# A new order of the TensorE step in a gated linear attention layer with a routed expert MLP

## The chip, the cores and the metric

The kernel is one program on one core of a Trainium2 chip. Its time is the device time of one execution in microseconds, the median of three runs. A profiled execution has its own time, and the span of its trace is a little shorter than that time.

## The reference

The input x holds 32 sequences of 256 tokens of 128 features. Each row is normalised, and two branches are added to it: a gated linear attention, and an MLP of which each token uses one expert of eight.

```
xn = layernorm(x)
q, k = xn @ Wq, xn @ Wk                 # 4 heads of 32
v, g = xn @ Wv, xn @ Wg                 # 4 heads of 64
gk   = log_sigmoid(xn @ Wgk + bgk) / 16 # one decay per token and head
o    = chunked gated linear attention of q, k, v, gk (causal, with a state per head)
on   = o * rsqrt(mean(o*o) + 1e-5) * gnorm_w
attn = (on * silu(g)) @ Wo
e    = argmax(softmax(xn @ gate_w))
ffn  = probability[e] * (gelu(xn @ w1[e] + b1[e]) @ w2[e] + b2[e])
out  = x + attn + ffn
```

## The kernel before, in words

The program is written engine by engine: each of the five engines has its own instruction list, in the order in which the source calls its helpers, and semaphores tie the lists together. Nothing is scheduled by a compiler.

There are three stages. The first loads x, transposes it and works out decays, router logits and the table that sorts tokens by expert. The second, the attention, takes one sequence a step, s = 0 to 31, in a pipeline over several steps. The third runs 71 blocks of 128 sorted rows through the MLP: TensorE multiplies, VectorE (`weigh`) makes the result and GpSimd adds it to the output rows by an indirect DMA with accumulation (`scatter`, L619). GpSimd starts its first scatter when the 32 attention results (`res`) have landed in the output, since it waits for `res_stored`.

In step s TensorE works on three sequences at once: Q and K (`proj_qk`, psQK) and V and G (`proj_vg`, psVG) of s+1; the transposed first keys (`first_keys`), the scores, the state and the outputs of s; the transposes of the normed outputs (`transpose_on`, psT) of s-1 and the last projection (`project_out`, psT) of s-2. Matmuls are fp32, so most of them appear as two records each; Q, K, V and G are three fp32r products each.

The scores of the four heads are four matmuls of 32 rows side by side. Two heads write psA and two write the first halves of psVG's two banks. So `scores(s)` waits until VectorE has read G of s out of psVG (`gate_ready`), and `proj_vg(s+1)`, which comes after it and overwrites psVG, waits until VectorE has read those scores (`p_ready`). The steps 6 to 29 are a loop of the sequencer with two steps in its body (L953).

ScalarE squares the outputs of s-1, copies the transposes of s-2, makes the eight decay tiles E of s+1 (`exp_dec`), copies Q and K of s+1, and then takes tanh of G and copies V. VectorE makes `gate`, `x_lo` (the low parts of x for s+2), the mean squares `ms` and `msn`, the masked scores `pr` (`probs`), the decayed keys `kd`, the gated outputs `og`, the scaled queries `qe`, the normed outputs `on`, the state `S_sb` and the residual `res`. GpSimd takes the power -1/2 (`rms`), masks E of s+1 (`mask_dec`, L554) once `on` of s-1 is made, and between these places sorted rows by indirect DMAs, two or three a step in the steps 5 to 29 (L577). SyncE issues the loads of decays and the stores of results.

In the last step, s = 31, the MLP's first blocks are mixed in, and the expert numbers are read into VectorE's registers (`value_load`, L1678).

Of the kernel before, what the change touches and what calls it, by code (L numbers as in the profile page):

```python
# [63 lines left out]
def build_layer(nc, x, Wq, Wk, Wv, Wg, Wgk, bgk, Wo, gnorm_w, gate_w, w1, b1, w2, b2, out):  # L64
# [40 lines left out]
    with ExitStack() as ctx:  # L105
# [99 lines left out]
        qk_sb = sb("qk_sb", [P, 2 * SEQ])  # L205
        kT = qk_sb[:, SEQ:2 * SEQ]
# [29 lines left out]
        psKS = ps("psKS", [P, 512])  # L236
        psA = ps("psA", [P, 2, 512])
        psO = ps("psO", [P, 512])
# [106 lines left out]
        BY_HALVES = (0, 1, LAST)  # L345
        HEADS_IN_TURN = (2, 3, 0, 1)
        ps_pair = [psA, psVG]
# [291 lines left out]
        def _(pe):  # L639
# [120 lines left out]
            def proj_vg(i, j):  # L760
                s = i * 2 + j
                parts = [(x_hi[j], w_hi), (x_hi[j], w_lo), (x_lo[j], w_hi)]
                if not (isinstance(i, int) and s == 0):
                    pe.wait_ge(v_copied, s)
                    pe.wait_ge(th_ready, s)
                    pe.wait_ge(gate_ready, s)
                    if not (isinstance(i, int) and s - 1 in BY_HALVES):
                        pe.wait_ge(p_ready, (s - 1) * 2 + 1)
# [5 lines left out]
            def first_keys(i, j):  # L774
                s = i * 2 + j

                pe.wait_ge(qk_copied, s + 1)
                nc.tensor.transpose(psKS[:, 0:P], kT[:, 0:P], ident[:]).then_inc(k0_ready, 1)


            def scores(i, j):
                s = i * 2 + j
                pe.wait_ge(p_ready, s * 2)
                pe.wait_ge(gate_ready, s + 1)
                if isinstance(i, int) and s == SLOTS_AT + 1:
                    pe.wait_ge(slot_read, 2)
                for k in range(2):
                    for h in HEADS_IN_TURN:
                        rows_h = slice(h * DK, (h + 1) * DK)
                        last = nc.tensor.matmul(ps_pair[h // 2][:, h % 2, k * P:(k + 1) * P], kT[rows_h, k * P:(k + 1) * P], qk_sb[rows_h, k * P:(k + 1) * P],  # L790
# [5 lines left out]
            def scores_by_halves(i, j):  # L796
# [3 lines left out]
                for k in range(2):  # L800
                    for r in range(2):
                        rows_r = slice(r * 2 * DK, (r + 1) * 2 * DK)
                        last = nc.tensor.matmul(psA[:, r, k * SEQ:(k + 1) * SEQ].rearrange("p (b t) -> p b t", b=2), kT[rows_r, k * P:(k + 1) * P], qb[rows_r, :, k * P:(k + 1) * P],
# [4 lines left out]
            def state(i, j):  # L808
# [3 lines left out]
                pe.wait_ge(v_copied, s + 1)  # L812
                for c in range(2):
                    last = nc.tensor.matmul(psKS[c * 2 * DK:(c + 1) * 2 * DK, HV:HV + 2 * DV], kd[:, c * 2 * DK:(c + 1) * 2 * DK],  # L814
# [3 lines left out]
            def own_half(i, j, k):  # L818
                s = i * 2 + j
                if k == 0:  # L820
                    pe.wait_ge(p_ready, (s + 1) * 2)
                for h in range(H):
                    for c in range(2):
                        t = k * SEQ + h % 2 * P + c * P // 2
                        nc.tensor.matmul(psO[c * P // 2:(c + 1) * P // 2, k * HV + h * DV:k * HV + (h + 1) * DV], pr[:, h // 2, t:t + P // 2],  # L825
                                         v_sb[j][:, k, h * DV:(h + 1) * DV], start=(k == 0 and h == 0), stop=False,
                                         skip_group_check=True)

            def outputs(i, j):
# [4 lines left out]
                own_half(i, j, 0)  # L834
                own_half(i, j, 1)
# [26 lines left out]
            def project_out(i, j):  # L862
                s = i * 2 + j
                pe.wait_ge(oT_copied, s + 1)
                for k in range(2):
                    for a in range(2):
                        last = nc.tensor.matmul(psT[:, k * D:(k + 1) * D], oT[:, 2 * k + a, :], wo_sb[:, a, :],  # L867
# [3 lines left out]
            def step(i, j, extra=None, ahead_of_outputs=None):  # L871
                first_keys(i, j)
                proj_qk(*turn(i, j, 1, 2))
                scores(i, j)
# [3 lines left out]
                proj_vg(*turn(i, j, 1, 2))  # L878
# [4 lines left out]
                transpose_on(*turn(i, j, -1, 2))  # L883
# [63 lines left out]
            transpose_on(0, 0)  # L947
# [5 lines left out]
            with pe.Fori(3, SEQS // 2 - 1) as i:  # L953
# [52 lines left out]
            scores_by_halves(last, 1)  # L1006
# [12 lines left out]
            project_out(last, 0)  # L1019
# [3 lines left out]
            project_out(last, 1)  # L1023
# [13 lines left out]
        def _(act):  # L1037
# [758 lines left out]
```

## Time and profile before

| what | us |
| --- | --- |
| median of three runs (389.52 to 390.5) | 389.59 |
| profiled execution | 389.28 |
| span of its trace | 387.5 |
| TensorE busy | 373.4 (96%) |
| VectorE busy | 314.5 (81%) |
| ScalarE busy | 291.8 (75%) |
| GpSimd busy | 279.1 (72%) |

Times in the rows are microseconds from the start of the span, and PE, DVE, ACT and POOL are TensorE, VectorE, ScalarE and GpSimd. Ends of matmuls are modelled in the profile, and matmuls overlap, so the time of a group of matmuls is best read from its start to the start of the next group; a busy TensorE is not one at its peak. What ended an engine's idle time stands in brackets.

### The profile page before, as it was taken

How to read it: one execution, taken by the hardware profiler on the slowest of the kernel's cores; microseconds unless marked ns; L12 is line 12 of the kernel's file. 1: busy time of each engine (PE TensorE's matmuls, PEld its weight loads, DVE VectorE, ACT ScalarE, POOL GpSimd, SP SyncE). 2: the span in 40 equal slices, each digit the busy share in tenths (PEclk: the TensorE clock that was granted, in tenths of full speed). 3: DMA queues.
4: the chain of work that ended last, by engine and by line, in shares of the span. 5: the costliest groups of instructions: out<-in, count | busy, mean ns of one | idle time of the engine just before them, and what ended most of it. 6: DMA issues, size and time to landing. Idle time of an engine off the chain costs nothing.

```text
span 387.5 us, 13901 instructions
## 1 busy us (share of the span) xinstructions
PE 373.4 (96%) x3963; PEld 321.2 (83%) x3963; DVE 314.5 (81%) x859; ACT 291.8 (75%) x889; POOL 279.1 (72%) x245
## 2 busy tenths in 40 slices
PE   7999999999999999999999999899999999999992
PEld 7667777777777877787777877899999999999991
DVE  5988999989898988888888878777788787777761
ACT  4889987788888888888888886566666667666661
POOL 8003534878787888888788873288888888888886
PEclk9999999999999999999999999999999999999997
DMA  8946788456555445575654423155555455556440
GB/s 231 257 140 198 223 270 292 134 170 191 170 184 161 138 147 157 158 200 162 191 157 150 131 79 81 54 67 72 64 72 70 65 70 71 69 71 76 75 37 6
DMA packets 59106, 51.45 MB, mean 133 GB/s; under 512 B 7200, under 2 KB 51392, under 8 KB 59072
## 3 DMA queue, kind: packets, MB, share of 16 engines
q1 hardware_dynamic: 45936, 42.07, 38.8%
q0 software_dynamic: 12272, 8.54, 15.3%
q10 hardware_dynamic: 864, 0.40, 0.4%
q8 instruction: 20, 0.33, 0.4%
q14 instruction: 14, 0.11, 0.1%
HBM read 33.14 MB, written 18.30 MB: 133 GB/s over the span
## 4 chain that ended last, share of the span: by engine, by line
PE 83%; DVE 4%; DMA 3%; issue 3%; ACT 2%; POOL 2%; SPq 2%; DVEq 0%; ACTq 0%; POOLq 0%
PE psA L988 16%; PE psVG L976 15%; PE psVG L771 11%; PE psT L867 8%; PE psO L825 7%; PE psQK L757 5%; PE psT L851 4%; PE psVG L790 4%; PE psO L839 3%; PE psKS L814 3%; POOL out_dram L619 2%; SPq L355 2%; DMA x_all<-in_L_attn_x_dram 1%; ACT E L1160 1%; DMA gcB<-decay_rows 1%
## 5 line engine op out<-in xcount | busy, mean ns | idle before, releaser
L619 POOL DMA_INDIRECT out_dram<-yw,sidx x71 | 112.9, 1590 | 28.8 <-DVE sidx L1700 17.5
L1160 ACT ACTIVATE E<-gcB,ngc 128x128 f32<-128x128 f32 x256 | 78.3, 395 | 0.7 <-DMA gcB<-decay_rows 0.7
L577 POOL DMA_INDIRECT sorted_rows<-x_all,pos_i x64 | 64.9, 1015 | 13.4 <-issue 12.8
L561 POOL TENSOR_TENSOR rms<-msn,neg_half 128x8 f32<-128x8 f32 x32 | 54.4, 1699 | 26.5 <-DVE msn L1492 22.5
L554 POOL TENSOR_SCALAR_AFFINE_SELECT E<-E 128x1024 f32<-128x1024 f32 x32 | 35.2, 1099 | 36.5 <-ACT E L1160 24.9
L1142 ACT ACTIVATE th<-psVG,x_all 128x256 f32<-128x256 f32 x64 | 26.9, 470 | 20.4 <-issue 11.6
L988 PE MATMUL psA<-xT_all,v_sb 128*128 x288 | 38.3, 276 | 1.0 <-issue 0.6
L976 PE MATMUL psVG<-xgT,gcB 128*128 128x128 f32 x288 | 37.9, 275 | 0.0
L988 PE MATMUL psA<-xT_all,th 128*128 x280 | 37.4, 276 | 0.0
L976 PE MATMUL psVG<-xgT,E 128*128 128x128 f32 x280 | 37.0, 275 | 0.0
L867 PE MATMUL psT<-wo_sb,oT 128*128 128x128 f32 x256 | 36.9, 287 | 0.0
L825 PE MATMUL psO<-v_sb,pr 128*64 128x64 f32 x1024 | 35.4, 222 | 1.0 <-DVE pr L1521 0.8
L988 PEld LDWEIGHTS psA<-xT_all,v_sb 128*128 128x128 f32 x288 | 35.0, 192 | 1.4 <-issue 1.4
L825 PEld LDWEIGHTS psO<-v_sb,pr 128*64 128x64 f32 x1024 | 34.1, 138 | 1.6 <-issue 1.5
L976 PEld LDWEIGHTS psVG<-xgT,gcB 128*128 128x128 f32 x288 | 35.0, 192 | 0.0
L988 PEld LDWEIGHTS psA<-xT_all,th 128*128 128x128 f32 x280 | 34.0, 192 | 0.3 <-issue 0.2
L976 PEld LDWEIGHTS psVG<-xgT,E 128*128 128x128 f32 x280 | 34.1, 192 | 0.0
L867 PEld LDWEIGHTS psT<-wo_sb,oT 128*128 128x128 f32 x256 | 31.0, 191 | 3.7 <-issue 0.2
L1169 ACT ACTIVATE sq<-psO 128x512 f32<-128x512 f32 x32 | 19.2, 600 | 13.8 <-PE psO L839 12.5
L771 PE MATMUL psVG<-w_hi,x_hi 128*128 128x512 f32 x64 | 28.2, 441 | 0.9 <-DVE pr L1526 0.6
L1563 DVE SCALAR_TENSOR_TENSOR gate<-th,psVG 128x512 f32<-128x512 f32 x32 | 22.0, 688 | 8.1 <-issue 4.6
L1704 DVE TENSOR_SCALAR yw<-yb,xg 128x128 f32<-128x128 f32 x71 | 26.1, 368 | 2.5
(214 smaller groups left out, 950.6 us busy)
## 6 DMA issues: line engine op xcount, KB each, us to landing
gcB<-decay_rows SPq DMA_DIRECT2D x32, 512.0 KB
sorted_rows<-blank SPq DMA_DIRECT2D x12, 396.0 KB, 5.0
xg<-sorted_rows SPq DMA_DIRECT2D x71, 66.0 KB
x_all<-in_L_attn_x_dram SPq DMA_DIRECT2D x16, 256.0 KB, 5.2
out_dram<-res SPq DMA_DIRECT2D x32, 128.0 KB
eqB<-decay_exp_rows SPq DMA_DIRECT2D x32, 64.0 KB
w1b<-in_L_ffn_w_dram SPq DMA_DIRECT2D x8, 256.0 KB
xT_all<-in_L_ffn_w_dram SPq DMA_DIRECT2D x32, 64.0 KB
```

Source lines behind the costliest of these rows:

```text
L554: nc.gpsimd.affine_select(out=E[j][:], in_=E[j][:], pattern=[[0, 2 * H], [1, P]], compare_op=ALU.is_ge, fill=0.0, base=0, channel_multipli ...
L561: nc.gpsimd.tensor_tensor(rms[j][:], msn[j][:], neg_half[:, 0:2 * H], ALU.pow).then_inc(rms_ready, 1)
L577: nc.gpsimd.indirect_dma_start(out=sorted_dram, out_offset=bass.IndirectOffsetOnAxis(ap=pos_i[:, t:t + 1], axis=0), in_=x_all[:, t, :], in ...
L619: nc.gpsimd.indirect_dma_start(out=out_rows, out_offset=bass.IndirectOffsetOnAxis(ap=sidx[j][:], axis=0), in_=yw[j][:], in_offset=None, bo ...
L771: last = nc.tensor.matmul(psVG[:, k, :], xp[:, k * P:(k + 1) * P], wp[:, 2 * P:], start=(n == 0), stop=(n == 2))
L825: nc.tensor.matmul(psO[c * P // 2:(c + 1) * P // 2, k * HV + h * DV:k * HV + (h + 1) * DV], pr[:, h // 2, t:t + P // 2], v_sb[j][:, k, h * ...
L867: last = nc.tensor.matmul(psT[:, k * D:(k + 1) * D], oT[:, 2 * k + a, :], wo_sb[:, a, :], start=(a == 0), stop=(a == 1))
L976: last = nc.tensor.matmul(psVG[:, j % 2, c * P:(c + 1) * P], wbuf[j % 4][:, c * P:(c + 1) * P], xgT[j % 2][:], start=True, stop=True)
L988: last = nc.tensor.matmul(psY[j % 2][:, 0:D], hid[j % 2][:, c, :], w2_sb[:, bass.ds(e, 1), c, :].rearrange("p a d -> p (a d)"), start=(c = ...
L1142: last = nc.scalar.activation(th[:, k, :], psVG[:, k, HV:2 * HV], ACT.Tanh, scale=x_all[:, bass.ds(s * 2 + k, 1), D + 2:D + 3].rearrange(" ...
L1160: last = nc.scalar.activation(E[j][:, k, h * P:(h + 1) * P], gcB[j][:, k * H + h, :], ACT.Exp, bias=ngcf[:, bass.ds((s * 2 + k) * H + h, 1)])
L1704: c_y.up(nc.vector.tensor_scalar(yw[j][:], yb[j % 2][:], xg[j][:, D:D + 1], None, ALU.mult))
```

## The change

TensorE's step gets another order. Transposes of normed outputs move from the end of the step to behind Q and K and take the sequence s-2 there, one step later than before. V and G come ahead of the scores. The scores leave psVG: psKS and psO become the two banks of one tensor psKO, and the pair of heads that wrote psVG now writes the second half of each of those two banks, the other pair the first halves of psA. The state moves to columns 128 to 255 of psKS. Q and K get two buffers in SBUF.

So the waits move as well. `proj_vg` no longer waits for `p_ready`. `scores(s)` waits for `og` of s-1, for the state copy of s-1 and for `kd` of s, which read the banks that it writes. `state(s)` waits for the first half of `pr`, and `outputs(s)` does the two pairs of heads one after the other, each behind its half of `pr`.

`project_out` is cut in halves of 64 columns of the stationary operand, so it has eight matmuls for four; in the last two sequences the old form stays (`project_whole`). The loop over TensorE's steps 6 to 29 is written out. Step 31 uses the ordinary scores.

VectorE and ScalarE get orders to match: VectorE makes `og` and `kd` ahead of `ms`, and `S_sb` ahead of `on`; ScalarE copies Q and K right behind the squares, and makes E in two halves, one on each side of tanh and V. The first two expert numbers are read in step 30 instead of behind it.

The first place is TensorE's step in the loop of before, the first instruction of each group with its waits (keys, Q and K, scores, projection, V and G, state, outputs of the own chunk, outputs from the state, transposes):

```order
L778 MATMUL psKS<-ident,qk_sb 128x128 [waits qk_copied]
L757 MATMUL psQK<-x_hi,w_hi 128x256 [waits qk_copied,qe_ready,lo_ready,hi_ready]
L790 MATMUL psVG<-qk_sb 128x128 [waits gate_ready,p_ready]
L867 MATMUL psT<-wo_sb,oT 128x128 [waits oT_copied]
L771 MATMUL psVG<-w_hi,x_hi 128x512 [waits p_ready]
L814 MATMUL psKS<-v_sb,kd 64x128 [waits v_copied,kd_ready]
L825 MATMUL psO<-v_sb,pr 64x64 [waits p_ready]
L839 MATMUL psO<-S_sb,qe 64x256 [waits qe_ready,s_copied]
L851 MATMUL psT<-ident,on 128x128 [waits res_ready,dve_on]
```

The same place now:

```order
L776 MATMUL psKO<-ident,qk_sb 128x128 [waits qk_copied]
L757 MATMUL psQK<-x_hi,w_hi 128x256 [waits qk_copied,qe_ready,lo_ready,hi_ready]
L855 MATMUL psT<-ident,on 128x128 [waits res_ready,dve_on]
L769 MATMUL psVG<-w_hi,x_hi 128x512 [waits gate_ready,th_ready,v_copied]
L790 MATMUL psKO<-qk_sb 128x128 [waits s_copied,kd_ready,og_ready,p_ready]
L872 MATMUL psT<-wo_sb,oT 64x128 [waits oT_copied]
L816 MATMUL psKO<-v_sb,kd 64x128 [waits p_ready,v_copied,kd_ready]
L826 MATMUL psKO<-v_sb,pr 64x64 [waits p_ready,og_ready]
L843 MATMUL psKO<-S_sb,qe 64x256 [waits qe_ready,s_copied]
```

Transposes and V and G now stand between Q and K and the scores, and only the projection is left between the scores and the state.

The second place is VectorE's step 9, the last before its own loop (which keeps the same order). Before:

```order
L1563 SCALAR_TENSOR_TENSOR gate<-th,psVG 128x512 [waits th_ready,v_copied]
L1348 TENSOR_TENSOR x_lo<-xT_all,x_hi 128x256 [waits hi_ready]
L1488 TENSOR_REDUCE ms<-sq 128x8 [waits sq_ready]
L1492 SCALAR_TENSOR_TENSOR msn<-ms,vpe 128x8 [waits rms_ready,dve_ms]
L1526 TENSOR_TENSOR pr<-psVG,E 128x2x2x128 [waits a_ready,o_ready,e_masked]
L1526 TENSOR_TENSOR pr<-psA,E 128x2x2x128 [waits a_ready]
L1532 TENSOR_TENSOR kd<-psKS,e_k 128x128 [waits k0_ready]
L1538 TENSOR_TENSOR og<-psO,gate 128x512 [waits sq_ready]
L1511 TENSOR_TENSOR qe<-psQK,eqB 128x128 [waits o_ready,qk_copied,eqB_loaded0]
L1546 TENSOR_TENSOR on<-og,rms 128x512 [waits oT_ps_ready,rms_ready,og_ready]
L1554 TENSOR_TENSOR S_sb<-psKS,headmask 128x256 [waits o_ready,s_ready]
L1571 TENSOR_TENSOR res<-psT,x_all 128x256 [waits res_stored1,wo_ready]
```

Now:

```order
L1587 SCALAR_TENSOR_TENSOR gate<-th,psVG 128x512 [waits th_ready,v_copied]
L1370 TENSOR_TENSOR x_lo<-xT_all,x_hi 128x256 [waits hi_ready]
L1562 TENSOR_TENSOR og<-psKO,gate 128x512 [waits dve_on,sq_ready]
L1554 TENSOR_TENSOR kd<-psKO,e_k 128x128 [waits k0_ready]
L1510 TENSOR_REDUCE ms<-sq 128x8 [waits sq_ready]
L1514 SCALAR_TENSOR_TENSOR msn<-ms,vpe 128x8 [waits rms_ready,dve_ms]
L1533 TENSOR_TENSOR qe<-psQK,eqB 128x128 [waits o_ready,qk_copied,eqB_loaded0]
L1548 TENSOR_TENSOR pr<-psKO,E 128x2x2x128 [waits a_ready,o_ready,e_masked]
L1548 TENSOR_TENSOR pr<-psA,E 128x2x2x128 [waits a_ready]
L1578 TENSOR_TENSOR S_sb<-psKO,headmask 128x256 [waits o_ready,s_ready]
L1570 TENSOR_TENSOR on<-og,rms 128x512 [waits oT_ps_ready,rms_ready,og_ready]
L1595 TENSOR_TENSOR res<-psT,x_all 128x256 [waits res_stored1,wo_ready]
```

`og` and `kd` stand ahead of the masked scores, `ms` behind them both, and the state ahead of `on`.

The diff, cut to its core:

```diff
@@ setup
-        qk_sb = sb("qk_sb", [P, 2 * SEQ])
-        kT = qk_sb[:, SEQ:2 * SEQ]
+        qk_sb = [sb(f"qk_sb{j}", [P, 2 * SEQ]) for j in range(2)]
+        kT = [t[:, SEQ:2 * SEQ] for t in qk_sb]
...
-        psKS = ps("psKS", [P, 512])
+        psKO = ps("psKO", [P, 2, 512])
+        psKS, psO = psKO[:, 0, :], psKO[:, 1, :]
         psA = ps("psA", [P, 2, 512])
-        psO = ps("psO", [P, 512])
...
-        BY_HALVES = (0, 1, LAST)
+        BY_HALVES = (0, 1)
-        ps_pair = [psA, psVG]
+        ps_scores = [psA[:, :, 0:SEQ], psKO[:, :, SEQ:2 * SEQ]]
@@ tensor
             def scores(i, j):
                 pe.wait_ge(p_ready, s * 2)
-                pe.wait_ge(gate_ready, s + 1)
+                pe.wait_ge(og_ready, s)
+                pe.wait_ge(s_copied, s)
+                pe.wait_ge(kd_ready, s + 1)
...
             def state(i, j):
                 pe.wait_ge(kd_ready, s + 1)
                 pe.wait_ge(v_copied, s + 1)
+                if not (isinstance(i, int) and s in BY_HALVES):
+                    pe.wait_ge(p_ready, s * 2 + 1)
...
             def outputs(i, j):
-                own_half(i, j, 0)
-                own_half(i, j, 1)
+                first, second = (0, 1) if isinstance(i, int) and s in BY_HALVES else (1, 0)
+                pe.wait_ge(p_ready, s * 2 + 1)
+                own_pair(i, j, first, True)
+                pe.wait_ge(p_ready, s * 2 + 2)
+                own_pair(i, j, second, False)
...
             def project_out(i, j):
                 for k in range(2):
                     for a in range(2):
+                        for c in range(2):
+                            last = nc.tensor.matmul(psT[c * P // 2:(c + 1) * P // 2, k * D:(k + 1) * D], oT[:, 2 * k + a, c * P // 2:(c + 1) * P // 2],
+                                                    wo_sb[:, a, :], start=(a == 0), stop=(a == 1), skip_group_check=True)
...
             def step(i, j, extra=None, ahead_of_outputs=None):
                 first_keys(i, j)
                 proj_qk(*turn(i, j, 1, 2))
+                transpose_on(*turn(i, j, -2, 2))
+                proj_vg(*turn(i, j, 1, 2))
                 scores(i, j)
                 project_out(*turn(i, j, -2, 2))
                 if extra:
                     extra()
-                proj_vg(*turn(i, j, 1, 2))
                 state(i, j)
                 if ahead_of_outputs:
                     ahead_of_outputs()
                 outputs(i, j)
-                transpose_on(*turn(i, j, -1, 2))
...
-            transpose_on(0, 0)
...
-            with pe.Fori(3, SEQS // 2 - 1) as i:
+            for i in range(3, SEQS // 2 - 1):
...
             first_keys(last, 1)
-            scores_by_halves(last, 1)
+            scores(last, 1)
+            transpose_on(last - 1, 1)
@@ scalar, step
+                if inside(i, j, 1, SEQS):
+                    copy_qk(*turn(i, j, 1, 2))
                 if inside(i, j, -2, SEQS):
                     copy_oT(*turn(i, j, -2, 2))
                 if inside(i, j, 1, SEQS):
-                    exp_dec(*turn(i, j, 1, 2))
-                    copy_qk(*turn(i, j, 1, 2))
+                    exp_half(*turn(i, j, 1, 2), 0)
...
                     tanh(*turn(i, j, 1, 2))
                     copy_v(*turn(i, j, 1, 2))
+                    exp_half(*turn(i, j, 1, 2), 1)
@@ vector
-            step(last, 0)
+            step(last, 0, aside=load_first_experts)
...
-            dve.wait_ge(w_loaded, W_LOADS * 16)
-            e0, e1 = expert_of(0, 0), expert_of(0, 1)
+            e0, e1 = first_experts
```

## Rows read from the trace of the kernel before

**Rows 1.** The page: chain that ended last, shares of the span by engine.

```profile
PE 83%; DVE 4%; DMA 3%; issue 3%; ACT 2%; POOL 2%; SPq 2%; DVEq 0%; ACTq 0%; POOLq 0%
```

**Rows 2.** Windows: stretch in us, its length, busy time of each engine, clock, DMA.

```profile
78.50:228.30 149.80, 149.37 (x1865) 118.89 (x1864) 129.54 (x277) 126.28 (x344) 122.23 (x105) 1.00 0.56 163
```

**Rows 3.** Timeline of TensorE, one step and a half: start, length, engine, line, what, count.

```profile
130.45 0.27 PE L778 MATMUL psKS<-ident,qk_sb 128*128 128x128 f32 x1
130.48 0.36 PE L757 MATMUL psQK<-x_hi,w_hi 128*128 128x256 f32 x1
...
132.03 1.16 PE L867 MATMUL psT<-wo_sb,oT 128*128 128x128 f32 x8
133.13 0.50 PE L771 MATMUL psVG<-w_hi,x_hi 128*128 128x512 f32 x1
...
133.69 0.39 PE L771 MATMUL psVG<-w_hi,x_lo 128*128 128x512 f32 x1
...
134.40 0.39 PE L771 MATMUL psVG<-w_hi,x_lo 128*128 128x512 f32 x1
134.72 0.44 PE L814 MATMUL psKS<-v_sb,kd 128*64 128x128 f32 x4
134.99 1.10 PE L825 MATMUL psO<-v_sb,pr 128*64 128x64 f32 x32
...
136.98 0.32 PE L778 MATMUL psKS<-ident,qk_sb 128*128 128x128 f32 x1
137.31 0.36 PE L757 MATMUL psQK<-x_hi,w_hi 128*128 128x256 f32 x1
...
138.18 0.38 PE L790 MATMUL psVG<-qk_sb 32*128 32x128 f32 x2
...
138.84 1.16 PE L867 MATMUL psT<-wo_sb,oT 128*128 128x128 f32 x8
139.75 0.48 PE L771 MATMUL psVG<-w_hi,x_hi 128*128 128x512 f32 x1
```

**Rows 4.** Timeline of VectorE in the same stretch, with what ended its idle time.

```profile
130.39 0.66 DVE L1348 TENSOR_TENSOR x_lo<-xT_all,x_hi 128x256 fp32r<-128x256 f32 x1
...
132.38 0.69 DVE L1526 TENSOR_TENSOR pr<-psVG,E 128x512 f32<-128x512 f32 x1
...
133.59 0.28 DVE L1532 TENSOR_TENSOR kd<-psKS,e_k 128x128 f32<-128x128 f32 x1
...
134.82 0.68 DVE L1546 TENSOR_TENSOR on<-og,rms 128x512 f32<-128x512 f32 x1
...
136.30 0.69 DVE L1563 SCALAR_TENSOR_TENSOR gate<-th,psVG 128x512 f32<-128x512 f32 x1
136.91 0.42 DVE L1348 TENSOR_TENSOR x_lo<-xT_all,x_hi 128x256 fp32r<-128x256 f32 x1
...
138.94 0.69 DVE L1526 TENSOR_TENSOR pr<-psVG,E 128x512 f32<-128x512 f32 x1 [0.64 <-PE psA L790]
```

**Rows 5.** Timeline of GpSimd in the same stretch.

```profile
125.47 1.67 POOL L561 TENSOR_TENSOR rms<-msn,neg_half 128x8 f32<-128x8 f32 x1 [0.54 <-DVE msn L1492]
...
129.65 1.11 POOL L554 TENSOR_SCALAR_AFFINE_SELECT E<-E 128x1024 f32<-128x1024 f32 x1
...
132.40 1.67 POOL L561 TENSOR_TENSOR rms<-msn,neg_half 128x8 f32<-128x8 f32 x1 [0.49 <-DVE msn L1492]
...
138.46 1.67 POOL L561 TENSOR_TENSOR rms<-msn,neg_half 128x8 f32<-128x8 f32 x1 [0.29 <-DVE msn L1492]
```

**Rows 6.** Timeline of all engines in step 31, where the MLP begins.

```profile
236.51 0.68 DVE L1538 TENSOR_TENSOR og<-psO,gate 128x512 f32<-128x512 f32 x1
...
237.11 1.28 DVE L1521 TENSOR_TENSOR pr<-psA,E 128x512 f32<-128x512 f32 x2
```

**Rows 7.** Timeline of GpSimd: the first and the last of its 71 scatters.

```profile
251.61 1.65 POOL L619 DMA_INDIRECT out_dram<-yw,sidx  x1 [7.44 <-DVE sidx L1700]
...
384.29 1.56 POOL L619 DMA_INDIRECT out_dram<-yw,sidx  x1 [0.30 <-issue]
```

More of the change, by code:

```diff
@@ L789, in scores @@
                         rows_h = slice(h * DK, (h + 1) * DK)
[L790 removed]
+                        last = nc.tensor.matmul(ps_scores[h // 2][:, h % 2, k * P:(k + 1) * P], kT[j][rows_h, k * P:(k + 1) * P], qk_sb[j][rows_h, k * P:(k + 1) * P],
                                                 start=True, stop=True)
@@ L812, in state, with own_pair @@
                 pe.wait_ge(v_copied, s + 1)
+                if not (isinstance(i, int) and s in BY_HALVES):
+                    pe.wait_ge(p_ready, s * 2 + 1)
                 for c in range(2):
-                    last = nc.tensor.matmul(psKS[c * 2 * DK:(c + 1) * 2 * DK, HV:HV + 2 * DV], kd[:, c * 2 * DK:(c + 1) * 2 * DK],
+                    last = nc.tensor.matmul(psKS[c * 2 * DK:(c + 1) * 2 * DK, P:P + 2 * DV], kd[:, c * 2 * DK:(c + 1) * 2 * DK],
                                             v_sb[j][:, 0, c * 2 * DV:(c + 1) * 2 * DV], start=True, stop=True)
                 last.then_inc(s_ready, 1)
[L818 to L827, printed above, removed]
+            def own_pair(i, j, r, first):
+                for k in range(2):
+                    for h in (2 * r, 2 * r + 1):
+                        for c in range(2):
+                            t = k * SEQ + h % 2 * P + c * P // 2
+                            nc.tensor.matmul(psO[c * P // 2:(c + 1) * P // 2, k * HV + h * DV:k * HV + (h + 1) * DV], pr[:, r, t:t + P // 2],
+                                             v_sb[j][:, k, h * DV:(h + 1) * DV], start=(first and k == 0 and h == 2 * r), stop=False,
+                                             skip_group_check=True)
             def outputs(i, j):
@@ L866, in project_out, with project_whole @@
                     for a in range(2):
+                        for c in range(2):
+                            last = nc.tensor.matmul(psT[c * P // 2:(c + 1) * P // 2, k * D:(k + 1) * D], oT[:, 2 * k + a, c * P // 2:(c + 1) * P // 2],
+                                                    wo_sb[:, a, :], start=(a == 0), stop=(a == 1), skip_group_check=True)
+                last.then_inc(wo_ready, 1)
+            def project_whole(i, j):
+                s = i * 2 + j
+                pe.wait_ge(oT_copied, s + 1)
+                for k in range(2):
+                    for a in range(2):
                         last = nc.tensor.matmul(psT[:, k * D:(k + 1) * D], oT[:, 2 * k + a, :], wo_sb[:, a, :],
@@ L1018, in _ @@
             layer2(0, 0, expert_of(0))
-            project_out(last, 0)
+            project_whole(last, 0)
             transpose_last_on()
@@ L1022, in _ @@
             pe.wait_ge(res_ready, SEQS - 1)
-            project_out(last, 1)
+            project_whole(last, 1)
             transpose_rows(0, 3)
@@ L1537, in gated @@
                 dve.wait_ge(sq_ready, s + 1)
+                if not (isinstance(i, int) and s == 0):
+                    dve.wait_ge(dve_on, s)
                 nc.vector.tensor_tensor(og[:].rearrange("p k n -> p (k n)"), psO[:], gate[j][:].rearrange("p k n -> p (k n)"), ALU.mult).then_inc(og_ready, 1)
```

65 lines of the change are left out of this document (37 added, 28 removed).

## The prediction

> **What bounds the kernel now.** I read the chain of waits first. TensorE holds 83% of it [rows 1], so next I read the windows of the attention's regular part: 149.80 us for the steps 7 to 29, which are 23, so 6.513 us a step, with TensorE busy for 149.37 of them at a granted clock of 1.00, the 2.4 GHz level [rows 2]. A busy TensorE is not one that waits for nothing, so I went on to its timeline and took each group from its start to the start of the next [rows 3]. Two kinds of step alternate there. In the first, Q and K follow the keys after 130.48 - 130.45 = 0.03 us, but V and G start 133.13 - 132.03 = 1.10 after the projection. In the second the distances are 137.31 - 136.98 = 0.33 and 139.75 - 138.84 = 0.91. So the one loses 0.19 ahead of V and G and the other 0.30 behind its keys. The 0.19 is the wait for VectorE's first `pr`, which starts at 132.38, 0.75 before V and G [rows 4]; the 0.30 comes in one step of the two in the loop's body, so I put it down to the loop's branch.
>
> Behind the attention GpSimd sets the time. Its first scatter starts at 251.61 after an idle time of 7.44, and its last ends at 384.29 + 1.56 = 385.85, 134.2 later [rows 7]; idle time of 0.30 ahead of the last is its own issue. Nothing of the change touches that stage, so the end moves by as much as the first scatter moves. That one waits for the residual of s = 31, the end of the attention's tail.
>
> I count against the profiled execution, 389.28 us (span 387.5 and 1.8 around it). The median of the runs is 0.31 higher.
>
> **The steps.** (a) Waits that go. V and G no longer share psVG with scores, and the loop is written out. Mean of the two kinds: (0.19 + 0.30)/2 = 0.245 us a step less. If a written-out list has a price of its own, it would be as large as the branch at most, so this term lies between 0.095 and 0.245.
>
> (b) Switches of the tile's shape. The last matmul of V and G starts at 134.40 and the state, in 64-column tiles, at 134.72, 0.32 later; the last four of the six matmuls of V and G start (134.40 - 133.69)/3 = 0.237 apart [rows 3]. I take 0.32 - 0.237 = 0.085 for a switch. Before, a step has four (into the scores, out of them, into the state, out of the outputs); afterwards three (into the scores, from there to half projections, out of the outputs to the keys), as half projections, state and outputs have 64 columns alike. 0.085 less, between nothing and that.
>
> (c) The projection in halves has 16 records for 8, and no row shows it. Undisturbed, the whole form takes 0.91 [rows 3]. The nearest row is the state, whose four records of the same 128 elements, two and two side by side in 64-column tiles, take 134.99 - 134.72 = 0.27, its first pair with the switch [rows 3]: some 0.11 for a pair. Eight pairs: 0.88, plus 0.04 of start, 0.92. Against the mean of the whole form without its wait, 0.99 with the switch out of the scores counted, that is 0.07 less. Were halves to run one after the other, 16 times 0.11 = 1.76, and the step would be 0.8 longer. I take the state's row, which has the same tile and length.
>
> The Trainium skill (TensorEngine Tiling (Array Packing), Restrictions) says that column tiling switches off Fast Weight Load, which would speak against (c). The trace shows no such price in the state's 0.27 [rows 3]; if each half paid for a visible load, it would be the serial case above.
>
> The step: 6.513 - 0.245 - 0.085 - 0.07 = 6.11, 0.40 less.
>
> **Waits that are new, at 6.11 a step.** `state` and `outputs` now stand behind `pr` with only the projection in between. The first `pr` starts 138.94 - 138.18 = 0.76 after the scores [rows 3, 4], and 0.75 later TensorE went on from it: 1.51. Scores (138.84 - 138.18 = 0.66) and the projection (0.92) fill 1.58. A slack of 0.07 is thin; each 0.1 that VectorE is later costs 2.9 us in all. Behind a waiting state stand outputs and the next step's keys, so such a wait is paid in full. The second `pr` ends about 0.6 behind the first, while the state (0.27) and one pair of outputs (half of the 136.98 - 134.99 = 1.99 that outputs and transposes take, at the least 0.4) run.
>
> The scores wait for `og` and `kd`. `og` can start when the outputs end, which is where the next keys start; ahead of the scores stand keys, Q and K (138.18 - 137.31 = 0.87), transposes (0.5, an estimate from those 1.99) and V and G (1.59), 3.0 in all. `gate` (0.61 to the next start), `x_lo` (0.42 to 0.66) and `og` and `kd` (0.68 and 0.28) are 2.0 to 2.3 [rows 4, 6]. Slack about 0.8: nothing.
>
> VectorE in a ring from scores to scores: 0.76 to `pr`, 1.28 for two of them [rows 6], state and `res` taken as `x_lo`'s 0.42 each (256 elements too), `on` 0.68, then the 2.0 to 2.3: 5.6 to 5.9. Below 6.11.
>
> `x_lo` takes 0.66 beside GpSimd's `select` of 129.65 to 130.76 and 0.42 without it [rows 4, 5]. The Trainium skill (SBUF — State Buffer, SBUF: two separate sides) has these two lock each other out of a shared port for a whole instruction. The trace agrees in direction; by that rule `x_lo` would be held in every step now, as `select` always follows `on` directly, and 0.24 to 0.6 more fit into the slack of 0.8, so the sum stays.
>
> GpSimd: the time from `rms` to `rms` is 132.40 - 125.47 = 6.93 with three sorting DMAs and 138.46 - 132.40 = 6.06 with two; without the idle time ahead of the second, 0.49 and 0.29, that is 6.44 and 5.77, mean 6.10 [rows 5]. This is the same as the step that I forecast. Steps with two give back what those with three lose, by way of `on`, which has slack; I charge nothing here and keep it as the first rival.
>
> ScalarE and SyncE get no more work: ScalarE is busy for 129.54 of 149.80 [rows 2], 5.63 a step.
>
> **The tail.** In step 31 before, `og` starts at 236.51 and the first `pr` at 237.11, 0.60 later, since its scores were made long before [rows 6]. Now `og` (0.68), then scores, then 0.76: about 1.5, so 0.9 later. The transposes and the projection of s = 29, moved back by a step, stand in front as well: about 0.5 + 0.92 less what fills that wait. I take +1.85 together, between +0.5 (all of it hidden but the later transposes) and +2.5 (all in line). Reading two expert numbers in step 30 goes onto VectorE where TensorE is waited for; I take 0.3, between nothing and `og`'s 0.68.
>
> **Sum.** 29 steps (2 to 30) times 0.40 = 11.7 less; 1.85 + 0.3 more: 389.28 - 9.6 = 379.7, and 380.0 beside the median.
>
> **Rivals.** First, GpSimd's ring binds in the 25 steps in which it sorts. For it: its mean of 6.10 without any idle time. Steps with three DMAs then take 6.44 and those with two at least TensorE's 6.11, of which some is made up: about 6.25. 25 times 0.14 = 3.5 more: 383.5.
>
> Second, slower: GpSimd's handover to VectorE. `ms` now stands behind `og` and `kd`, and `rms` waits for it. If GpSimd still idles ahead of `rms` in each step as it does now, by 0.29 to 0.54 [rows 5], and `kd`'s 0.28 comes on top, the ring is (6.93 + 6.06)/2 + 0.28 = 6.78, through `rms`, `on`, `select`, E and `pr`. 25 times 0.27 = 6.7 more, four other steps 1.6 less, tail 2.1 more: 396.8. It decides once the step is over 6.513 - 2.15/29 = 6.44. Against it: those idle times end with `msn` of a VectorE that is paced by TensorE, and shrink when the step does.
>
> Third, also slower: halves of the projection run serially, +0.8 in each step from (c): 380 + 29 x 0.84 = 404.
>
> Fourth, the change moves the wait but doesn't remove it: `state` waits for `pr` as V and G did, 0.2 to 0.3 a step, and the step stays at 6.4 to 6.45: 388 to 390. For it: the slack of 0.07. Against it: `pr` now stands behind short work (`ms`, `qe`), which the scores cover.
>
> **Chances.** The forecast 0.60, its own range 377.5 to 382.5 (step 6.04 to 6.18); below it 0.06 (VectorE's wait in outputs hides more, step 5.95, 375.5); first rival 0.20; fourth 0.06; second 0.05; third 0.03. A range of 375.5 to 386.5 leaves out the last three and a little at either end. A measurement of this kernel can tell 0.3%, 1.2 us, from no change. Faster: 0.60 + 0.06 + 0.20 and a third of the fourth, 0.87; the same 0.04; slower 0.09.
>
> **What would show it.** In the changed profile the windows of the steps 7 to 29 give 6.1 us a step; V and G follow the transposes without a gap; keys and Q and K are 0.03 apart in each step; the half projections take some 0.92 from start to the state's start, and the state doesn't wait for `pr` longer than 0.1. GpSimd idles ahead of `rms` less than 0.3. The first scatter starts at about 242, and in step 31 the first `pr` is 1.5 behind `og`. The forecast is wrong if the step is 6.2 or more; then what ended TensorE's idle time ahead of state or scores tells whether `pr` (fourth), E and GpSimd (first, second) or the projection itself (third) was it. It is wrong in the tail if the step is right and the first scatter is over 1 us off.

## The result, and the profile after

The changed kernel takes 401.55 us (400.1 to 401.76) beside 389.55 for the kernel before in the same session: 1.0296 times as long, 95% interval 1.0266 to 1.0326. Faster was forecast, 380.0, and the range ended at 386.5. The span grew from 387.5 to 399.4, so all of the 12 us is in the trace.

The chain of waits of the kernel after, shares of the span by engine, beside the 83% of TensorE before [rows 1]:

```profile
PE 50%; DVE 13%; issue 13%; ACT 10%; DMA 4%; POOL 3%; ACTq 2%; SPq 1%; DVEq 1%; another core or an unknown queue 1%; POOLq 0%
```

TensorE no longer sets the time alone. The windows of its steps 7 to 29 (stretch, length, busy time of TensorE, its weight loads, VectorE, ScalarE and GpSimd, granted clock, DMA):

```profile
79.00:234.85 155.85, 146.60 (x2049) 116.70 (x2047) 139.79 (x277) 126.21 (x344) 131.32 (x104) 1.00 0.58 158
```

155.85 / 23 = 6.776 us a step, against 6.513 [rows 2]. The clock is 1.00 as before, but TensorE now idles for 9 us of it. Its timeline, a step and a half, shows where (start, length, what; idle time and its end in brackets):

```profile
139.78 0.33 PE L776 MATMUL psKO<-ident,qk_sb 128*128 128x128 f32 x1
...
140.67 0.60 PE L855 MATMUL psT<-ident,on 128*128 128x128 f32 x4
141.09 0.47 PE L769 MATMUL psVG<-w_hi,x_hi 128*128 128x512 f32 x1
...
143.29 0.38 PE L790 MATMUL psKO<-qk_sb 32*128 32x128 f32 x2 [0.55 <-DVE kd L1554]
...
143.94 1.10 PE L872 MATMUL psT<-wo_sb,oT 128*64 128x128 f32 x16
145.18 0.44 PE L816 MATMUL psKO<-v_sb,kd 128*64 128x128 f32 x4
...
146.92 0.33 PE L776 MATMUL psKO<-ident,qk_sb 128*128 128x128 f32 x1
...
148.16 0.48 PE L769 MATMUL psVG<-w_hi,x_hi 128*128 128x512 f32 x1
...
149.73 0.38 PE L790 MATMUL psKO<-qk_sb 32*128 32x128 f32 x2
...
150.38 1.09 PE L872 MATMUL psT<-wo_sb,oT 128*64 128x128 f32 x16
151.59 0.44 PE L816 MATMUL psKO<-v_sb,kd 128*64 128x128 f32 x4
...
153.35 0.33 PE L776 MATMUL psKO<-ident,qk_sb 128*128 128x128 f32 x1
```

Steps of 7.14 and 6.43 alternate. In the long one V and G start at 141.09 and the scores at 143.29, 2.20 later; in the short one that distance is 149.73 - 148.16 = 1.57, so the scores of the long step wait 0.63 for `kd`. In both the state starts 1.21 to 1.24 behind the projection, which needs 0.94 (run 5 below), so it waits 0.3 for `pr`. VectorE at the same time:

```profile
140.87 1.48 DVE L1370 TENSOR_TENSOR x_lo<-xT_all,x_hi 128x256 fp32r<-128x256 f32 x1
142.26 0.68 DVE L1562 TENSOR_TENSOR og<-psKO,gate 128x512 f32<-128x512 f32 x1
142.86 0.28 DVE L1554 TENSOR_TENSOR kd<-psKO,e_k 128x128 f32<-128x128 f32 x1
143.06 0.67 DVE L1510 TENSOR_REDUCE ms<-sq 128x8 f32<-128x512 f32 x1
143.87 0.17 DVE L1514 SCALAR_TENSOR_TENSOR msn<-ms,vpe 128x8 f32<-128x8 f32 x1
...
144.35 0.68 DVE L1548 TENSOR_TENSOR pr<-psKO,E 128x512 f32<-128x512 f32 x1
...
147.53 0.42 DVE L1370 TENSOR_TENSOR x_lo<-xT_all,x_hi 128x256 fp32r<-128x256 f32 x1
...
150.76 0.69 DVE L1548 TENSOR_TENSOR pr<-psKO,E 128x512 f32<-128x512 f32 x1 [0.56 <-PE psA L790]
```

And GpSimd:

```profile
137.57 1.67 POOL L561 TENSOR_TENSOR rms<-msn,neg_half 128x8 f32<-128x8 f32 x1
139.43 1.50 POOL L577 DMA_INDIRECT sorted_rows<-x_all,pos_i  x1 [0.20 <-issue]
140.95 1.10 POOL L554 TENSOR_SCALAR_AFFINE_SELECT E<-E 128x1024 f32<-128x1024 f32 x1
142.23 0.97 POOL L577 DMA_INDIRECT sorted_rows<-x_all,pos_i  x1 [0.18 <-issue]
144.20 1.67 POOL L561 TENSOR_TENSOR rms<-msn,neg_half 128x8 f32<-128x8 f32 x1 [0.99 <-DVE msn L1514]
...
151.15 1.67 POOL L561 TENSOR_TENSOR rms<-msn,neg_half 128x8 f32<-128x8 f32 x1
```

In the long step `x_lo` takes 1.48 where it stood at 0.42 and 0.66 [rows 4], since it meets `select`; `og` and `kd` come 1.06 later for it. `rms` comes later too: `ms` and `msn` stand behind them, and GpSimd idles for 0.99 ahead of the `rms` of 144.20. In the other step GpSimd goes from `rms` to `rms` in 6.95 without waiting for anyone, with three sorting DMAs.

Together these two stretches are a closed ring: `rms` (137.57), the first DMA, `select`, `x_lo` (which ends at 142.35, 0.30 behind `select`), `og`, `kd`, `ms`, `msn`, `rms` (144.20), and from there GpSimd's own work up to the next `rms` (151.15). It takes 6.63 + 6.95 = 13.58 for two steps, 6.79 a step, and no instruction of TensorE is on it. So in these steps TensorE waits for a ring of GpSimd and VectorE.

The tail lost the rest. Keys, then scores of step 31:

```profile
241.79 0.33 PE L776 MATMUL psKO<-ident,qk_sb 128*128 128x128 f32 x1
245.00 0.58 PE L790 MATMUL psKO<-qk_sb 32*128 32x128 f32 x2 [2.88 <-DVE og L1562]
```

And the windows behind them (columns as above):

```profile
246.00:248.00 2.00, 2.00 (x18) 1.27 (x11) 1.29 (x2) 0.67 (x2) 0.00 (x0) 0.50 0.70 188
248.00:250.00 2.00, 2.00 (x24) 2.00 (x24) 1.80 (x5) 1.56 (x3) 0.46 (x1) 0.50 0.00 0
```

TensorE idled for 2.88 us, and the granted clock then fell to 0.50, its 1.2 GHz level, where it stayed until about 251. The first scatter comes at 263.31, 21.52 behind the keys of step 31; before it was 16.35 (251.61 less 235.26).

The account of 11.7 us at the first scatter: 0.5 up to step 7 (step 6 of 7.8 us gave back what had been won), 6.05 in the steps 7 to 29, nothing in step 30, 5.2 in the tail.

### The profile page after: what moved, and what is told of

Read it like the earlier page. It is cut to its first block, busy times and chain, and to the rows that moved or that the text cites. A ratio compares the mean times of both kernels' runs of the same rounds, so it can differ in the third digit from the quotient of the medians.

```text
span 399.4 us, 14355 instructions
## 1 busy us (share of the span) xinstructions
PE 371.4 (93%) x4211; PEld 319.8 (80%) x4211; DVE 325.3 (81%) x859; ACT 291.0 (73%) x887; POOL 289.4 (72%) x245
## 4 chain that ended last, share of the span: by engine, by line
PE 50%; DVE 13%; issue 13%; ACT 10%; DMA 4%; POOL 3%; ACTq 2%; SPq 1%; DVEq 1%; another core or an unknown queue 1%; POOLq 0%
PE psA L1001 15%; PE psVG L989 15%; ACT E L1175 6%; PE psKO L826 3%; DVE og L1562 3%; PE psQK L757 2%; DVE ms L1510 2%; DVE pr L1548 2%; PE psVG L769 2%; PE psKO L816 2%; PE psT L872 2%; ACT sq L1189 2%; POOL out_dram L619 2%; PE psKO L843 2%; DMA x_all<-in_L_attn_x_dram 1%
## 5 line engine op out<-in xcount | busy, mean ns | idle before, releaser
L577 POOL DMA_INDIRECT sorted_rows<-x_all,pos_i x64 | 74.8, 1169 | 13.5 <-issue 11.4
L1175 ACT ACTIVATE E<-gcB,ngc 128x128 f32<-128x128 f32 x256 | 82.1, 406 | 0.8 <-DMA gcB<-decay_rows 0.8
L1189 ACT ACTIVATE sq<-psKO 128x512 f32<-128x512 f32 x32 | 19.2, 601 | 32.0 <-PE psKO L843 22.4
L826 PE MATMUL psKO<-v_sb,pr 128*64 128x64 f32 x1024 | 37.3, 226 | 0.0
L826 PEld LDWEIGHTS psKO<-v_sb,pr 128*64 128x64 f32 x1024 | 35.9, 140 | 0.5 <-issue 0.2
L872 PE MATMUL psT<-wo_sb,oT 128*64 128x128 f32 x480 | 33.7, 284 | 0.0
L790 PEld LDWEIGHTS psKO<-qk_sb 32*128 32x128 f32 x240 | 16.5, 189 | 21.3 <-issue 21.3
L790 PE MATMUL psKO<-qk_sb 32*128 32x128 f32 x240 | 22.0, 300 | 10.0 <-DVE kd L1554 4.7
L872 PEld LDWEIGHTS psT<-wo_sb,oT 128*64 128x64 f32 x480 | 26.3, 139 | 3.7 <-ACT oT L1196 0.2
L1548 DVE TENSOR_TENSOR pr<-psKO,E 128x512 f32<-128x512 f32 x30 | 20.6, 688 | 9.5 <-PE psA L790 8.7
```

Source lines behind the costliest of these rows:

```text
L577: nc.gpsimd.indirect_dma_start(out=sorted_dram, out_offset=bass.IndirectOffsetOnAxis(ap=pos_i[:, t:t + 1], axis=0), in_=x_all[:, t, :], in ...
L790: last = nc.tensor.matmul(ps_scores[h // 2][:, h % 2, k * P:(k + 1) * P], kT[j][rows_h, k * P:(k + 1) * P], qk_sb[j][rows_h, k * P:(k + 1) ...
L872: last = nc.tensor.matmul(psT[c * P // 2:(c + 1) * P // 2, k * D:(k + 1) * D], oT[:, 2 * k + a, c * P // 2:(c + 1) * P // 2], wo_sb[:, a, ...
L1175: last = nc.scalar.activation(E[j][:, k, h * P:(h + 1) * P], gcB[j][:, k * H + h, :], ACT.Exp, bias=ngcf[:, bass.ds((s * 2 + k) * H + h, 1)])
L1548: nc.vector.tensor_tensor(pr[:, r, :].rearrange("p (k b t) -> p b k t", k=2, b=2), ps_scores[r].rearrange("p b (k t) -> p b k t", k=2), E[ ...
```

## The experiments

Steps are times from keys to keys, means of the steps 7 to 29. Kernels without sorted rows have an MLP without its data, so only their attention is read.

**1. x_lo behind the queries.**

```diff
-                if inside(i, j, 2, SEQS):
-                    split_lo(*turn(i, j, 2, 2))
                 if inside(i, j, -1, SEQS):
                     gated(*turn(i, j, -1, 2))
...
                     scale_q(*turn(i, j, 1, 2))
+                if inside(i, j, 2, SEQS):
+                    split_lo(*turn(i, j, 2, 2))
```

> VectorE makes x_lo behind the scaled queries instead of ahead of og, nothing else. Theory A (x_lo, 1.48 us beside GpSimd's select in every other step, makes og, kd and so the scores late): the 0.62 us that the scores wait in every other step goes, steps of 7.13 and 6.45 become about 6.45 and 6.45, the 25 steps are some 7.5 us shorter in all, 394 us. Theory B (GpSimd's own work with three sorting DMAs sets the pace, and x_lo is only seen to be long because VectorE waits anyway): the pair of steps stays at 13.6 us and the time at 400 to 402.

404.34 us, 1.040 times the kernel before (1.0383 to 1.0418), step 6.946. `x_lo` took 0.42 in every step, and yet the steps alternate between 6.15 and 7.7. Theory A alone falls. What came in its place, from the timeline of one step:

```profile
147.64 0.63 PE L843 MATMUL psKO<-S_sb,qe 128*64 128x256 f32 x4
...
148.20 0.33 PE L776 MATMUL psKO<-ident,qk_sb 128*128 128x128 f32 x1
...
148.33 0.96 POOL L577 DMA_INDIRECT sorted_rows<-x_all,pos_i  x1 [0.30 <-DVE on L1570]
...
150.16 0.60 ACT L1189 ACTIVATE sq<-psKO 128x512 f32<-128x512 f32 x1 [2.03 <-remote]
...
150.79 0.69 DVE L1562 TENSOR_TENSOR og<-psKO,gate 128x512 f32<-128x512 f32 x1 [1.89 <-ACT sq L1189]
```

The outputs' last matmuls start before 148.0 and TensorE goes on with keys and with Q and K, but ScalarE's squares, which wait for the outputs, start at 150.16. In the trace's semaphore events the increment of `o_ready` is at 149.95, 1.68 behind the modelled end of its matmul, and those of keys and of Q and K follow within 0.11, late as well. The three groups of matmuls end between 148.27 and 149.28, beside GpSimd's issues of indirect DMAs (at 146.99 for 1.04 and at 148.33 for 0.96), and their increments arrive some 1.65 behind the start of the second of them. The trace doesn't hold every increment. In the steps 7 to 29 of this run it holds 91 of TensorE's 113 whose matmul ends further than 1.7 us behind the start of such a DMA, and none of these is over 0.1 late; of the 82 that it holds within 1.7 us 49 are, by up to 1.8; of VectorE's and ScalarE's, inside or outside, none. That is theory C of the runs that follow.

**2. og and kd first in step 31.**

```diff
-            make_gate(last, 1)
-            norm_rows(0, 0)
-            copy_w(0, 0, e0)
-            decay_k(last, 1)
             gated(last, 0)
+            decay_k(last, 1)
+            make_gate(last, 1)
+            norm_rows(0, 0)
+            copy_w(0, 0, e0)
             probs(last, 1)
```

> In step 31 VectorE makes og and kd first, ahead of gate and of the MLP's first rows. Theory A (the 5.2 us that the tail has grown by are the scores' wait for og, 2.9 us, and the half clock that follows it from 244.5 to 251): scores start about 1.6 us earlier after the first keys, the clock falls for a shorter time or not at all, the first scatter comes 1.6 to 5 us earlier, 396.5 to 400 us. Theory B (the tail waits for transposes and projections that were moved behind): no more than 0.5 us, 401.

397.34, 1.022 (1.0196 to 1.0243): theory A. The scores follow the keys after 1.77 and TensorE idles for half as long:

```profile
242.35 0.33 PE L776 MATMUL psKO<-ident,qk_sb 128*128 128x128 f32 x1
244.12 0.38 PE L790 MATMUL psKO<-qk_sb 32*128 32x128 f32 x2 [1.44 <-DVE kd L1554]
```

Its clock stays at 1.00:

```profile
246.00:248.00 2.00, 2.00 (x52) 2.00 (x53) 1.94 (x6) 1.71 (x4) 0.17 (x1) 1.00 0.69 192
```

From keys to the first scatter it is 17.67, 3.85 less. The step, untouched, is 6.776 again.

**3. Both.**

> Both edits, x_lo behind the queries and og first in step 31. If both causes are right and independent, the sum of the two gains: 389 to 392 us, about level with the kernel before. If theory B of the first holds, no better than the second run.

403.34, 1.0389 (1.0363 to 1.0415), step 6.938. Only the tail's gain is there: 17.43 from keys to the first scatter.

**4. Two sorting DMAs in each step**, the third left out (`if n == 3: place_rows(t + 1)` removed).

> The changed kernel with two sorting DMAs in every step: the third one of 14 steps is left out, so 14 of 64 tiles of rows are not sorted. The attention's steps are what is read. Theory A (the lock between x_lo and select): select now starts directly behind on in every step and holds x_lo each time, no step is shorter than VectorE's 6.6 to 6.7, mean 6.6 to 6.8 as now. Theory B (GpSimd's load): 1.2 us less in every other step of GpSimd, mean 6.2 to 6.4.

Mean 6.558, but of two kinds: 6.15 in the steps 10 to 13, then 6.70 on average to the end. In the first kind the first DMA starts at 101.16, takes 1.03, and `x_lo` takes 0.74. In the second it starts at 139.91, just behind VectorE's `on` (139.85), takes 1.52, `select` comes that much later, and `x_lo` takes 1.48 in every step. So theory A's number came true for one of two kinds of step in one execution. In the second kind the ring above closes within each step: GpSimd goes from `rms` to `rms` in 6.67 to 6.73, and the last 1.0 of it is idle, until `msn`.

**5 to 7. No sorting DMA**: in the changed kernel, with `x_lo` behind the queries, and in the kernel before.

```diff
-                if n:
-                    place_rows(t)
-                if n == 3:
-                    place_rows(t + 1)
...
-                if n:
-                    place_rows(t + n - 1)
```

> The changed kernel without any of GpSimd's 64 sorting DMAs (no row is sorted, so the MLP's part of the output is missing); the attention's steps are read. Theory A (x_lo is held by select, as with two sorts in every step, where each step took 6.7): select starts behind on at once, x_lo still meets it, the step is 6.2 to 6.7 and x_lo over 0.8. Theory B (GpSimd's load sets the pace): the step falls to TensorE's own 6.1 to 6.2. Theory C (TensorE's semaphore increments arrive up to 1.7 us late while GpSimd issues an indirect DMA): none of them is late by more than 0.1 us, the state waits for pr at most 0.1 us.

> x_lo behind the queries, and no sorting DMA. With both the hold and the late increments gone nothing but TensorE is left: 6.1 to 6.2 us a step in every step, against 6.93 with the sorts. Theory C: ScalarE's squares start right behind the outputs, where with the sorts they started 1.7 us late in every other step. If the step stays over 6.5, the order of VectorE itself (og and kd ahead of ms) is the cause.

> The kernel before without any sorting DMA. Theory C: its increments come late as well, but where TensorE isn't waited for; the step goes from 6.51 to 6.2 to 6.4, the p_ready wait shrinks and the loop's 0.15 us a step stay. If the sorts cost the old order nothing, 6.45 to 6.51.

Steps of 6.157, 6.155 and 6.312. The windows of the steps 7 to 29, of the changed kernel:

```profile
77.78:219.40 141.62, 141.62 (x2050) 115.78 (x2048) 131.57 (x278) 126.47 (x344) 62.82 (x47) 1.00 0.50 150
```

and of the kernel before:

```profile
78.20:223.37 145.17, 145.17 (x1865) 117.64 (x1864) 126.24 (x278) 126.23 (x345) 62.72 (x46) 1.00 0.49 145
```

TensorE waits in neither. The new kernel is 0.155 us a step shorter, as (b) and (c) had it together; `x_lo` still meets `select` in the changed kernel (0.72 in each step) and it costs nothing. So the sorts cost 6.513 - 6.312 = 0.20 a step before the change and 6.776 - 6.157 = 0.62 after it.

**8. x_lo ahead of gate** (and the tail of run 2).

> The changed kernel with x_lo ahead of gate and with og and kd first in step 31, all sorts in place. Theory A: in the steps in which x_lo met select it now ends before select starts, so scores wait 0.3 to 0.6 less there; mean step 6.5, 390 to 393 us. Theory C: which increments are late changes with the alignment and is not foreseen; if one of those for the outputs is late, as with x_lo behind the queries, the time is 397 or more.

412.76, 1.0621 (1.0575 to 1.0667), step 7.411: not theory A; it lies in the open range that theory C gave (397 or more), far above its lower end. In every other step `x_lo` still meets `select` (1.92) and now holds up `gate` with it, for which V and G wait up to 1.4; in the other steps the squares wait up to 2.2 as in run 1.

**9. Memsets for DMAs.** Each `place_rows` becomes two memsets on GpSimd, which keep it about as busy but issue no DMA.

> The changed kernel with two memsets (768 and 384 numbers a partition, together some 1.3 us with the wait between them) in the place of each sorting DMA on GpSimd, no row sorted; the attention's steps are read. Theory B (GpSimd's time is what the DMAs cost): the steps stay near 6.8, or 6.5 at the least. Theory C (TensorE's increments are held up by the issue of an indirect DMA, and only then): no increment of TensorE is over 0.1 us late and the step is 6.15 to 6.3, though GpSimd is as busy.

Step 6.155, and no increment of TensorE came late. The windows (GpSimd is the fifth busy time, 126.67 for 62.82 in run 5):

```profile
79.60:221.18 141.58, 141.58 (x2050) 115.73 (x2048) 128.34 (x278) 126.47 (x344) 126.67 (x163) 1.00 0.51 150
```

But a step with three pairs of memsets took GpSimd 6.26, not the 6.95 of three DMAs, so it didn't yet rule out GpSimd's time; run 13 does that.

**10 and 11. Two DMAs ahead of select** and the third behind it, in the changed kernel (with the tail of run 2) and in the kernel before.

```diff
                 if n:
                     place_rows(t)
-                if n == 3:
                     place_rows(t + 1)
...
-                if n:
-                    place_rows(t + n - 1)
+                if n == 3:
+                    place_rows(t + 2)
```

> The changed kernel with GpSimd's sorting DMAs two ahead of select in each step and the third behind it (before, one or two ahead and one behind), and with og and kd first in step 31. Theory A: select comes late enough in every step, x_lo takes 0.42 everywhere, the scores' wait goes: step 6.4 to 6.5, 388 to 390. Theory C: x_lo takes 0.42, but other increments come late, the outputs' above all, and the step is over 6.6 all the same: 394 to 400.

> The kernel before with the same order of sorting DMAs on GpSimd. Without any of them its step was 6.31 for 6.51, so 0.2 us a step can be had at most, 4.6 us in all. Theory C: the two-ahead order moves which increments are late; step 6.4 to 6.7, 387 to 393. If only GpSimd's total load counts, no change: 388 to 390.

392.99, 1.0085 (1.0049 to 1.0121), from ten runs between 391.54 and 398.21; and 397.06, 1.0172 (1.0116 to 1.0228), step 6.839. In the profiled execution of the first, which was the longest of the ten, steps of 6.25 and 6.6 stand for a while and then turn into 6.15 and 7.5; nothing rests on that. For the second only the place of the same DMAs has changed, and the step is 0.33 longer: GpSimd's load as such is no explanation.

**12. ms ahead of og and kd**, as before the change.

> The changed kernel with ms and msn ahead of og and kd in VectorE's step (as before), the rest unchanged. If the handover to GpSimd (rms behind msn) is the ring that binds, rms starts 0.9 us earlier and the step falls to 6.4 to 6.6. If it isn't, og and kd come 1.1 us later, the scores wait more in every step: 6.9 to 7.3, 404 to 412 us.

419.26 in its one run, step 7.599. `rms` no longer waits for `msn`, so the handover is off the ring, but the step went past both ranges that I had given: VectorE's state copy now waits up to 2.1 for late increments, and GpSimd's `select` up to 2.0 for the `on` behind it. Another wait has come in, so this run doesn't tell what the handover costs in the changed kernel.

**13. Longer memsets**, 768 and 640 numbers a partition.

> As the run with memsets, with 768 and 640 numbers a partition, so that GpSimd is held for some 1.45 us by each and as long as by a DMA (its step with three was 6.95 us from rms to rms with nothing idle). Theory B (GpSimd's time): the steps alternate again and their mean is 6.5 to 6.8. Theory C (late increments and the lock of a DMA, not GpSimd's time): 6.15 to 6.3, no increment of TensorE late.

Step 6.548, 6.94 and 6.15 in turn, with no increment of TensorE late: theory B, for 0.39 of the 0.62. GpSimd's step with three pairs, none of it idle, is now nearly as long as one with three DMAs, 6.89:

```profile
140.20 1.64 POOL L563 TENSOR_TENSOR rms<-msn,neg_half 128x8 f32<-128x8 f32 x1 [0.74 <-DVE msn L1523]
141.78 2.92 POOL L581 MEMSET blank<- 128x768 f32 x4
144.66 1.09 POOL L556 TENSOR_SCALAR_AFFINE_SELECT E<-E 128x1024 f32<-128x1024 f32 x1
145.69 1.43 POOL L581 MEMSET blank<- 128x768 f32 x2
147.09 1.64 POOL L563 TENSOR_TENSOR rms<-msn,neg_half 128x8 f32<-128x8 f32 x1
```

But `x_lo` is held here as well, in every other step, and `rms` waits 0.74 behind it:

```profile
137.28 1.07 DVE L1379 TENSOR_TENSOR x_lo<-xT_all,x_hi 128x256 fp32r<-128x256 f32 x1
```

So the 0.39 isn't the price of GpSimd's time alone, but of its time and the hold in the same ring, which takes 6.19 (from the `rms` of 134.01 to that of 140.20) + 6.89 = 13.08 here. With `x_lo` at 0.42 the ring would be 0.65 shorter, 6.2 a step, TensorE's own step or nearly so; that is an estimate from these rows, and no run has shown it.

**14 and 15. res ahead of on**, with the tail of run 2, and in the second with two DMAs ahead of `select`.

```diff
+                if not read and inside(i, j, -2, SEQS):
+                    residual(*turn(i, j, -2, 2))
                 if inside(i, j, -1, SEQS):
                     normed(*turn(i, j, -1, 2))
...
-                if inside(i, j, -2, SEQS):
+                if read and inside(i, j, -2, SEQS):
                     residual(*turn(i, j, -2, 2))
```

> The changed kernel with res ahead of on in VectorE's step, and og and kd first in step 31; all sorts in place. If an on that starts first stretches the first DMA from 1.03 to 1.50 us, on now starts 0.33 us later and the DMA takes 1.03 in every step, select moves ahead of x_lo's start, x_lo takes 0.7 to 1.0 instead of 1.48, and the scores' wait of 0.62 falls to 0.1 to 0.3: mean step 6.4 to 6.6, 388 to 393 us (397.3 without the edit). If not, 396 to 399; if the new alignment makes the outputs' increments late, over 400.

> The same with two sorting DMAs ahead of select. Its steps were 6.43 in a stretch of nine and 6.8 behind it. If on doesn't stretch the first DMA any more, GpSimd needs 6.5 and 5.5 us for its two kinds of step, and the step is 6.25 to 6.4 throughout: 386 to 390 us, level with the kernel before or better. If increments are late for another reason, 392 or more.

404.25, 1.0374 (1.034 to 1.0407), step 6.939; 417.59, 1.0717 (1.0682 to 1.0751), step 7.551. The first DMA took 1.03 in both and `x_lo` 1.05 instead of 1.48 in the first and 0.42 in the second, much as foreseen, and the times grew all the same. VectorE in the first of them:

```profile
149.70 0.42 DVE L1370 TENSOR_TENSOR x_lo<-xT_all,x_hi 128x256 fp32r<-128x256 f32 x1
151.98 0.69 DVE L1562 TENSOR_TENSOR og<-psKO,gate 128x512 f32<-128x512 f32 x1 [1.86 <-ACT sq L1189]
```

The outputs' increments now come 1.9 to 2.0 late, as in run 1, in every other step, and in the second kernel in every step. The short steps of the first are 6.24, so I put what remains down to late increments. No version beat the kernel before; the best, run 10, lies 0.85% behind it.

## Why the prediction was wrong

**Steps (b) and (c) came out in their sum.** Their 0.155 is the measured 6.312 - 6.157; no run parts the two, and the two kernels also differ in the loop. The half projections take 0.94 to the state's start where it doesn't wait (run 5); TensorE's own step is 6.15, 6.11 was forecast. The third rival (halves one after the other) is out.

**Step (a) was wrong.** I put 0.30 behind the keys down to the loop's branch and 0.19 ahead of V and G to a wait on `pr` that the new order removes. Run 7 has loop and wait, and without the sorts both distances shrink: its steps are 6.29 with keys and Q and K 0.03 apart in most, and V and G follow the projection after 0.91. So 0.20 of my 0.245 was the sorts' price, and the change leaves the sorts where they are. The 0.33 that I read was also the largest of the 23 steps; most of the others with a gap have 0.13 to 0.22.

**The charge of nothing for GpSimd was the step that failed most**, and with it the slack of 0.8 in which `x_lo` was to be hidden. I let the short step, 5.77 without its idle time, pay for the long one, 6.44 (the 5.77 still had 0.40 in it of waiting for `on`, ahead of the `select` of 135.70). In the changed kernel the long one takes 6.95, as the first DMA takes 1.50 in place of 1.03 when `on` starts just ahead of it. The short one takes 6.63, as it ends in a wait for `msn`, and `msn` stands behind an `x_lo` that was held for 1.06, not 0.24 to 0.6. I had set that hold against the scores' slack alone; `rms` waits for it too, and there it has no slack. So what I summed as three separate things, GpSimd's work, VectorE's order and the hold, stands in series on one ring of 13.58 for two steps, and that is the measured step. By run 13 a ring without DMAs, with 1.07 in place of 1.48 for `x_lo`, costs 0.39 of the 0.62; the first rival, GpSimd's ring, was sized at 0.14.

The Trainium skill (SBUF — State Buffer, Who interferes with whom) has a VectorE instruction with two SBUF inputs and a GpSimd one that reads SBUF exclude each other for the whole of an instruction. The trace agrees: 1.48 is 0.42 and nearly all of `select`'s 1.10. Where GpSimd has time to spare (run 5) `x_lo`'s 0.72 was indeed hidden.

**Late increments were in no step of the prediction at all.** In the changed kernel they make the first `pr` start 150.76 - 149.73 = 1.03 behind the scores in every other step, where 0.76 was counted, against a slack of 0.07. The `on` behind that `pr` starts only with the end of `rms`, though (at 152.91, after 0.33 of waiting), so by the trace they aren't on the ring that sets the step here. Run 13, where none is late, fits this: its ring is 0.50 shorter for two steps, which is the 0.23 a step that it leaves, and 0.44 of it lies between `rms` and the end of `x_lo`, where the DMA and the gap ahead of it take longer than the two memsets. That they cost nothing here is read from the trace and not tested alone. In the runs 1, 8, 12, 14 and 15 increments that a step waits for come 1.6 to 2.1 late, so edits that moved the ring's work ran into them.

**The tail** was forecast at 2.15 more and cost 5.2. I counted from `og` to `pr`, but not that in step 31 `og` stands behind two operations of the MLP, one of which waited for its rows until 243.35, nor that the idle TensorE would fall to half its clock. Run 2 gives 3.85 of it back.

Together: 23 steps of 0.67 over the forecast, 15.3; 2.5 in the steps before them (0.5 later where 2.0 earlier was forecast); 0.4 in step 30; 3.0 in the tail: 21.2 of the 21.55 missed. The second rival's ring of 6.78 is the measured 6.776 by luck. Its handover through `ms` is on the ring, but as a wait of 0.99 in one step of two, behind the held `x_lo`; it had a wait of 0.29 to 0.54 in each step and `kd`'s 0.28 on top. Its 396.8 lacks 4.7 of the time, most of it the tail's.

## What to carry to other kernels

When a waiting engine is relieved, follow its partners' work around until it closes, with the holds of one engine by another in it: here each of three sums left slack, and the ring that joins them had none. A mean over long and short steps holds only if the short one doesn't end in a wait. A small gap that shows in one step of two in a regular loop points to what itself alternates (here two or three DMAs), and leaving that work out for one run shows what it costs before anything is reordered. A wait placed where the bounding engine idles can cost its clock too.

## What was not expected of the hardware

While GpSimd issues an indirect DMA, TensorE's semaphore increments can arrive late, by up to 1.8 us in run 1 and 2.1 in run 12, where the matmul ends up to 1.7 us behind the DMA's start; VectorE's and ScalarE's did not (counted in run 1), and with memsets about as long, or no DMA, TensorE's did not. What holds them up no run here shows. The first sorting DMA behind `rms` takes about 1.50 us where VectorE's `on` starts up to 0.1 ahead of it, and 1.03 where it doesn't, in every step 7 to 29 of all kernels with sorts. And the same program with two DMAs a step ran at 6.15 and then at 6.70 a step in one execution (run 4), the one with the DMA ahead of `on`, the other with `on` ahead.
